# An attention and mixture-of-experts kernel: its opening in another order, the first expert's weights split earlier, list entries of 64 bytes

## The chip, the cores and the metric

One core of a Trainium2 chip runs the whole program. Its engines are TensorE (PE, matmuls), VectorE (DVE), ScalarE (ACT), GpSimd (POOL) and SyncE (SP), which only issues DMAs; ScalarE and GpSimd issue DMAs too. The engines run beside each other and meet at semaphores. The metric is the device time of one launch in microseconds, the median of several runs.

## The reference, cut to what matters

64 images of 224 x 224 x 3 are cut into 196 patches of 768 values and embedded to 192 features; with a class token that is 197 tokens an image, 12608 in all. Then come a causal attention with 12 heads of 16, a residual and a layer norm, and a layer of eight experts with two choices per token and a capacity:

```python
emb = concat([cls, patches(x / 255) @ W + b]) + pos_emb
h = layernorm(emb + attn(emb))                      # 12 heads, causal softmax
scores, idx = top_k(h @ Wg, 2); weights = softmax(scores)
for k in range(2):                                  # capacity = int(1.2 * N / 8)
    pos = cumsum(onehot(idx[:, k])) - 1; keep = pos < capacity
    buf[idx, pos] = token                           # one list of tokens per expert and choice
    xg = h[buf]; a = (xg @ W1)[..., :H] * silu((xg @ W1)[..., H:])
    out[buf] += w_k * (a @ W2)
y = layernorm(h + out)
```

## The kernel before, in words

The program has two blocks, `attention_block` and `expert_block`, with a barrier of all engines between them. Products that need precision split an operand into a rounded part (`_hi`) and the rest (`_lo = value - _hi`): an engine rounds, another subtracts.

**Attention.** Work goes by pairs of images (`NPAIR` = 32), 396 columns each. `run_bodies` calls `body(i, ...)` for i = 0 to 35 on each engine, each body with twelve steps `s`; the middle ones run in a hardware loop. A body works on several pairs at once, by stages: "E" embeds pair i + 1, stage 1 makes q and k of pair i, 2 the scores of i - 1, 3 and on softmax, values and projection, 4 the norm, the choice of experts and the slots of i - 3, 5 the scatter of list entries of i - 4. q and k are stored to DRAM (`store_qk`) and read back in another layout (`spread_q`, `spread_k`) by SP. `embed(p, ft, k0)` on TensorE multiplies six 128-row tiles (`KT`) with three products each, for two halves `ft` of the features, 18 matmuls a half; VectorE's `embedded(p, ft)` turns the sum into `ht`. It needs `x_hi` (ScalarE, `x_round`) and `x_lo` (GpSimd, `x_rest`).

**The opening** (before body 0). SP loads `wtok` (768 KB), `raw` (776 KB), the six tiles of x of pair 0 (198 KB each), `wp` (144 KB) and thirteen constants, in this order. `wtok` and `raw` are loaded into `vp`, the tiles that later hold the values. Everything waits for the last constant (`s_w`): TensorE then does four small products (L574 to L586: the mean of the gate weights, the gate folded into the projection, and bias products), VectorE what hangs on them, ScalarE rounds `wtok`, then `raw`, then x. VectorE subtracts `wtok_lo` and `wa_lo` one after the other (L783, L784), then clears `vp` (L791); TensorE starts to embed when both are ready (`s_wsplit`). ScalarE clears the expert lists in DRAM first of all (L457).

**The lists.** For each token and choice, an entry with the weight and the token's row is written to `d["lists"]` at its slot by an indirect DMA of GpSimd (L443), eight per pair: steps s with s % 3 != 2. There are 30720 slots; an entry has `ROW` = 2 words. GpSimd also raises the variance to -1/2 (`rstd`, L420) at step 4 of each body, and masks the softmax. VectorE's code of step 2 multiplies y by the reciprocals (L840), which come by a DMA from ScalarE.

**Experts.** 80 chunks (`NCH`) of 384 list slots, ten for each expert. For each chunk SP loads the entries (`load_entries`), GpSimd gathers the tokens' rows of 1 KB with three indirect DMAs (L1142), TensorE turns them (`turn_rows`, L1225), ScalarE and VectorE split them, TensorE multiplies (L1242, L1255), and GpSimd scatters the result with an adding DMA (L1162). The weights of an expert (1408 KB) are split in ten pieces (`parts`): GpSimd rounds, VectorE subtracts. For expert 0 all ten stand at the start of the block (L1151, L1331); for the others one piece per chunk. SP loads the raw weights of experts 0 and 1 after the first four loads of entries and `ident`, those of expert x + 2 in chunk 2 of expert x. A last part normalizes all tokens.

## Time and profile before

| what | value |
|---|---|
| runs, median (lowest to highest) | 2357.99 us (2357.78 to 2363.21), 3 runs |
| profiled execution | 2355.76 us |
| its span, first to last instruction | 2354.0 us |
| TensorE busy | 2140.5 us (91%) |
| VectorE, ScalarE, GpSimd busy | 1590.6, 1083.2, 1576.6 us |
| opening, to the first QK product | 36.77 us |
| barrier between the blocks, first load of the experts | 1364.40 us |

A row of the timeline has the start in us, the duration in us, engine, line, operation, output<-input, shape and count, and in brackets the engine's idle time before it and what released it. A row of windows has the stretch, its length, busy time (and count) of the engines, the granted TensorE clock (1.00 is 2.4 GHz, 0.50 is 1.2 GHz), the busy share of the DMA engines and GB/s.

### The profile page before, as it was taken

The numbers are of one execution on the slowest core, as the hardware profiler recorded it, in microseconds if no ns is written. First come the engines' busy times: TensorE is split into PE (matmuls) and PEld (weight loads), VectorE is DVE, ScalarE is ACT, GpSimd is POOL, SyncE is SP. The second block draws the span as 40 slices with busy tenths as digits, with TensorE's granted clock in tenths as the row PEclk, the third lists the DMA queues.
The fourth block names the chain that finished last, engine by engine and source line by source line (L and its number), as shares of the span: only waits on it lengthen the run. The fifth ranks groups of instructions, "written<-read, shape, count | busy, mean of one in ns | idle before, by whom it ended". The sixth has DMA issues, their size and how long they took to land. (4 is left out here: it accounts for less than half of the span.)

```text
span 2354.0 us, 48984 instructions
## 1 busy us (share of the span) xinstructions
PE 2140.5 (91%) x14772; PEld 2070.2 (88%) x14772; DVE 1590.6 (68%) x4287; ACT 1083.2 (46%) x2840; POOL 1576.6 (67%) x2326
## 2 busy tenths in 40 slices
PE   4999999999999999999999559999999999999990
PEld 4899898999989999999988459999999999999980
DVE  4577777877777777777777436666666666666556
ACT  2344444444444444444444225454545454544545
POOL 3356676767666767676765557777777777767666
PEclk9999999999999999999999679999999999999995
DMA  5658888776676565655643133201010101000338
GB/s 155 153 119 123 137 127 142 130 133 137 140 124 139 135 135 136 134 137 133 139 111 84 34 112 62 44 6 26 2 29 3 28 3 26 2 2 15 54 48 332
DMA packets 232530, 219.72 MB, mean 93 GB/s; under 512 B 91027, under 2 KB 212754, under 8 KB 231376
## 3 DMA queue, kind: packets, MB, share of 16 engines
q1 hardware_dynamic: 134800, 146.55, 26.7%
q10 hardware_dynamic: 43328, 56.78, 12.9%
q0 software_dynamic: 54272, 14.76, 5.1%
q8 instruction: 68, 1.11, 0.2%
q14 instruction: 62, 0.51, 0.1%
HBM read 152.91 MB, written 95.25 MB: 105 GB/s over the span
## 5 line engine op out<-in xcount | busy, mean ns | idle before, releaser
L1162 POOL DMA_INDIRECT x_tokens<-yout,e_entry x240 | 382.0, 1592 | 182.1 <-DVE yout L1348 133.5
L651 PE MATMUL Y<-p,vp 128*102 128x198 f32 x1536 | 361.0, 344 | 17.6 <-ACT ysb L482 13.0
L443 POOL DMA_INDIRECT expert_lists<-entry,slot x256 | 288.1, 1126 | 54.1 <-issue 54.1
L1363 DVE TENSOR_TENSOR a<-UP,gate 128x384 f32<-128x384 f32 x320 | 178.6, 558 | 211.7 <-ACT gate L1300 169.8
L487 ACT ACTIVATE p<-ST 128x396 f32<-128x396 f32 x384 | 191.7, 499 | 264.5 <-PE ST L623 247.9
L1255 PE MATMUL Y<-w,a_hi 128*128 128x384 f32 x960 | 304.4, 354 | 2.0 <-DVE a_lo L1353 2.0
L1142 POOL DMA_INDIRECT rows<-x_wide,e_entry x240 | 250.3, 1043 | 77.4 <-issue 72.4
L1300 ACT ACTIVATE gate<-GT 128x384 f32<-128x384 f32 x320 | 157.6, 492 | 290.1 <-PE UP L1242 267.8
L141 POOL TENSOR_TENSOR word_p<-word_p 1x1 f32<-1x1 f32 x416 | 85.8, 206 | 304.6 <-ACT p L489 295.3
L409 POOL TENSOR_TENSOR x_lo<-x,x_hi 128x396 fp32r<-128x396 f32 x192 | 208.2, 1086 | 91.1 <-ACT x_hi L465 89.0
L651 PEld LDWEIGHTS Y<-p,vp 128*102 128x102 f32 x1536 | 221.6, 170 | 32.2 <-issue 11.4
L829 DVE TENSOR_REDUCE rm<-S 128x2 f32<-128x256 f32 x384 | 161.7, 421 | 117.6 <-PE S L642 106.9
L832 DVE TENSOR_REDUCE rm<-S 70x2 f32<-70x396 f32 x384 | 213.9, 557 | 0.0
L629 PE MATMUL S<-k,q 96*128 96x128 f32 x768 | 185.8, 243 | 25.2 <-DVE rm L832 18.6
L1262 PE MATMUL Y<-w,a_lo 128*128 128x192 f32 x960 | 206.8, 256 | 0.0
L655 PE MATMUL Y<-p,vp 70*102 70x70 f32 x1536 | 191.8, 247 | 1.9 <-POOL p L431 1.9
L655 PEld LDWEIGHTS Y<-p,vp 70*102 70x102 f32 x1536 | 185.7, 171 | 3.0 <-POOL p L431 2.6
L629 PEld LDWEIGHTS S<-k,q 96*128 96x128 f32 x768 | 147.4, 192 | 40.4 <-DVE rm L832 28.3
L1255 PEld LDWEIGHTS Y<-w,a_hi 128*128 128x128 f32 x960 | 180.9, 189 | 2.3 <-DVE a_lo L1353 2.2
L849 DVE RECIPROCAL rd<-ysb 6x198 f32<-6x198 f32 x128 | 177.4, 1386 | 4.7 <-ACT ysb L482 0.8
L1348 DVE SCALAR_TENSOR_TENSOR yout<-Y,e_entry,ylo 128x192 f32<-128x192 f32 x240 | 100.3, 418 | 117.0 <-ACT ylo L1289 105.4
L1353 DVE TENSOR_TENSOR a_lo<-a,a_hi 128x384 fp32r<-128x384 f32 x320 | 178.3, 560 | 0.0
(181 smaller groups left out, 6400.1 us busy)
## 6 DMA issues: line engine op xcount, KB each, us to landing
x<-in_xt ACTq DMA_DIRECT2D x180, 198.0 KB
q<-qk_features SPq DMA_DIRECT2D x384, 74.2 KB
k<-qk_features SPq DMA_DIRECT2D x192, 148.5 KB
qk_features<-qk_hi SPq DMA_DIRECT2D x96, 198.0 KB
qk_features<-qk_lo SPq DMA_DIRECT2D x96, 198.0 KB
e_raw<-in_wexp SPq DMA_DIRECT2D x8, 1408.0 KB, 6.7
rb<-rd ACTq DMA_DIRECT2D x128, 74.2 KB
t_x<-x_tokens SPq DMA_DIRECT2D x15, 576.0 KB, 7.5
```

The costliest lines, as they stand in the source:

```text
L409: pool.tensor_tensor(x_lo[:, t], x[:, t], x_hi[:, t].bitcast(F32), ALU.subtract)\
L443: pool.indirect_dma_start(d["lists"][:, :], bass.IndirectOffsetOnAxis(ap=slot[o][0:REAL[t], t, c:c + 1], axis=0), entry[o][0:REAL[t], t, c ...
L487: act.activation(p32[b][:, :, 0:TI], ST[0][:, 0:TP].rearrange("p (h c) -> p h c", h=2), ACT.Exp, scale=SCALE)
L629: pe.matmul(S[0][:, b * P:(b + 1) * P], qt[rows, im, b, j, 0:P], kt[rows, im, j, 0:P], start=(b == 0), stop=False)
L651: return pe.matmul(Y[0:VW1, 0:TI], v0, p32[b][:, hh, 0:TI], start=start, stop=stop)
L655: pe.matmul(Y[0:VW1, P:TI], v1, p32[b][0:T1, hh, TI:TI + T1], start=False, stop=False)
L832: dve.tensor_reduce(rm[im][0:T1, 1, j:j + 7:6], S[1][0:T1, 0:TP].rearrange("p (h c) -> p h c", h=2), AX.X, ALU.max, negate=True).then_inc( ...
L1142: pool.indirect_dma_start(rows[cc % 2][:, t, :], None, d["xin"][:, :], row_of(cc, t), bounds_check=N - 1, oob_is_err=False).then_inc(s_row ...
L1162: pool.indirect_dma_start(d["x1"][:, :], row_of(cc, t), yout[q][:], None, bounds_check=N - 1, oob_is_err=False, compute_op=ALU.add)\
L1255: return pe.matmul(y[:, 0:2 * C], a_hi[q][:, m, c], w2[e][:, m].rearrange("p a b -> p (a b)"), start=(m == 0), stop=(m == HM - 1))
L1262: pe.matmul(y[:, 0:C], a_lo[q][:, m, c], w2[e][:, m, 0], start=False, stop=False)
L1363: dve.tensor_tensor(a32[m % 2][:], UP[m % 2][:, 0:TILE3], gate[m % 2][:], ALU.mult)\
```

## The change

Three edits are made together.

- **The opening.** SP loads wtok, the x of pair 0, raw, and seven constants that are needed later; `wp` and the other seven constants go by ScalarE's queue. wtok has its own semaphore. ScalarE rounds wtok and x before `raw`, and clears the lists last. VectorE subtracts `wtok_lo` first, and `wa_lo` only after the first half of the embedding. TensorE embeds the first half before the small products, which then stand between the parts of the second half. One of the two clearings of q goes to GpSimd, and the clearing of `vp` into body 0 at step 6.
- **The first expert's weights.** Tiles that attention no longer needs (x, x_hi, x_lo, ht, wtok_lo) become the first of the two sets of expert weights. SP loads the first expert's weights at the end of body 32; ScalarE rounds and VectorE subtracts them in body 34 at step 0. In that body GpSimd's `rstd` moves from step 4 to step 11. At the start of the expert block SP loads one expert's weights instead of two, and no second `ident`.
- **The entries** have 16 words (64 bytes) instead of 2; the lists grow from 240 KB to 1920 KB, and are cleared from a tile that is written ten times.

```diff
+ROW, BLANK = 16, 24
 XW = C + C - P
...
-        x = sb("x", [P, KT, TP], F32)
-        x_hi, x_lo = (sb(n, [P, KT, TP], F32R) for n in ("x_hi", "x_lo"))
...
-        loads = [(wpt, "wpt"), (wg, "wg"), (bpc, "bpc"), (bqk, "bqk"), (bv, "bv"), (bp, "bp"), (postab, "pos"),
-                 (biastab, "bias"), (ident, "ident"), (masks, "masks"), (iota8, "iota8"),
-                 (kbase, "kbase"), (valid, "valid"), (tid, "tid")]
+        loads = [(wpt, "wpt"), (wg, "wg"), (bpc, "bpc"), (bv, "bv"), (bp, "bp"), (postab, "pos"), (biastab, "bias")]
+        late_loads = [(bqk, "bqk"), (ident, "ident"), (masks, "masks"), (iota8, "iota8"), (kbase, "kbase"),
+                      (valid, "valid"), (tid, "tid")]
...
-            sp.dma_start(wtok, d["wtok"]).then_inc(s_w, 16)
-            sp.dma_start(raw, d["raw"]).then_inc(s_w, 16)
+            sp.dma_start(wtok, d["wtok"]).then_inc(s_tok, 16)
             for t in range(KT):
                 sp.dma_start(x[:, t], d["xt"][0][:, t]).then_inc(s_x, 16)
-            sp.dma_start(wp[0:CH, :, E:], d["wp"]).then_inc(s_w, 16)
-            for dst, name in loads:
+            sp.dma_start(raw, d["raw"]).then_inc(s_w, 16)
+            for dst, name in late_loads:
                 sp.dma_start(dst[:], d[name]).then_inc(s_w, 16)
...
+                if isinstance(i, int) and i == NPAIR:
+                    sp.wait_ge(s_ef, 2 * NPAIR)
+                    sp.wait_ge(s_xlo, KT * NPAIR)
+                    sp.wait_ge(s_hlo, 2 * NPAIR)
+                    shared.load_weights(sp, d, 0, 0)
...
+            pool.memset(q[1][:].bitcast(F32), 0.0).then_inc(s_qset, 1)
...
-                    if s == 4 and 4 in stages:
+                    if s == (11 if isinstance(i, int) and i == NPAIR + 2 else 4) and 4 in stages:
...
-            act.wait_ge(s_blank, 1)
-            act.dma_start(d["lists"].rearrange("(p a) c -> p (a c)", p=P),
-                          blank[:].rearrange("p a c -> p (a c)")).then_inc(s_clear, 16)
-            act.wait_ge(s_w, 16 * (len(loads) + 3))
+            act.dma_start(wp[0:CH, :, E:], d["wp"]).then_inc(s_w, 16)
+            for dst, name in loads:
+                act.dma_start(dst[:], d[name]).then_inc(s_w, 16)
+            act.wait_ge(s_tok, 16)
             act.activation(wtok_hi[:], wtok, ACT.Copy).then_inc(s_whi, 1)
-            act.wait_ge(s_wg, 2)
-            act.activation(wa_hi[:].rearrange("p a b -> p (a b)"), raw, ACT.Copy).then_inc(s_whi, 1)
...
+            act.wait_ge(s_w, LOADS)
+            act.wait_ge(s_wg, 2)
+            act.activation(wa_hi[:].rearrange("p a b -> p (a b)"), raw, ACT.Copy).then_inc(s_whi, 1)
+            act.wait_ge(s_blank, 1)
+            act.dma_start(d["lists"].rearrange("(p n a) c -> p n (a c)", p=P, a=BLANK),
+                          blank[:].rearrange("p a c -> p (a c)").unsqueeze(1)
+                          .broadcast_to([P, NSLOT // P // BLANK, BLANK * ROW])).then_inc(s_clear, 16)
...
+                            if isinstance(i, int) and i == 1:
+                                act.wait_ge(s_vset, 4)
...
+                    if isinstance(i, int) and i == NPAIR + 2 and s == 0:
+                        act.wait_ge(shared.s_raw[0], 48)
+                        for j in range(10):
+                            src, hi, _ = shared.parts(j, 0)
+                            act.activation(hi, src, ACT.Copy).then_inc(shared.s_whi, 1)
...
-            pe.wait_ge(s_w, 16 * (len(loads) + 3))
-            pe.wait_ge(s_set, SETS)
...
-            pe.wait_ge(s_wsplit, 1)
...
-            for ft in range(2):
-                for k0 in range(0, KT, 2):
-                    embed(0, ft, k0)
+            pe.wait_ge(s_toksplit, 1)
+            for k0 in range(0, KT, 2):
+                embed(0, 0, k0)
+            pe.wait_ge(s_w, LOADS)
+            pe.wait_ge(s_set, SETS)
+            for f in range(2):
+                mm = pe.matmul(G[0][:, 0:E], share[:], wg[:, f, :], start=(f == 0), stop=(f == 1))
+            mm.then_inc(s_avg, 1)
+            embed(0, 1, 0)
...
+            embed(0, 1, 2)
...
+            embed(0, 1, 4)
+            pe.wait_ge(s_wsplit, 1)
...
+            dve.memset(q[0][:].bitcast(F32), 0.0).then_inc(s_qset, 1)
             for n in range(2):
-                dve.memset(q[n][:].bitcast(F32), 0.0).then_inc(s_qset, 1)
+                dve.memset(y[n][CH:CH + 1, 0, :], 1.0).then_inc(s_qset, 1)
+            dve.wait_ge(s_whi, 1)
+            dve.tensor_tensor(wtok_lo[:], wtok, wtok_hi[:].bitcast(F32), ALU.subtract).then_inc(s_toksplit, 1)
             for n in range(2):
                 ins = dve.memset(k[n][ROWS_QK:ROWS_QK + 1].bitcast(F32), 1.0)
             ins.then_inc(s_qset, 1)
-            for n in range(2):
-                dve.memset(y[n][CH:CH + 1, 0, :], 1.0).then_inc(s_qset, 1)
-            dve.wait_ge(s_w, 16 * (len(loads) + 3))
+            dve.wait_ge(s_w, LOADS)
             dve.tensor_tensor(addend[:], postab[:], biastab[:], ALU.add).then_inc(s_const, 1)
             dve.tensor_copy(bvs[:], bv[:].unsqueeze(2).broadcast_to([CH, 2, P])).then_inc(s_const, 1)
             dve.tensor_copy(bps[:], bpc[:].unsqueeze(2).broadcast_to([CH, 2, P])).then_inc(s_const, 1)
+            dve.wait_ge(s_const, 1)
+            embedded(0, 0)
             dve.wait_ge(s_avg, 1)
             gates = raw.rearrange("p (a b) -> p a b", a=2)[:, :, 3 * C:3 * C + E]
             dve.tensor_tensor(gates, gates, repeat(G[0][:, 0:E], 2), ALU.subtract).then_inc(s_wg, 1)
...
-            dve.tensor_tensor(wtok_lo[:], wtok, wtok_hi[:].bitcast(F32), ALU.subtract)
...
-            dve.wait_ge(s_wsplit, 1)
-            for n in range(2):
-                dve.memset(vp[n][:], 0.0).then_inc(s_vset, 1)
-            dve.wait_ge(s_vset, 2)
-            for n in range(2):
-                dve.memset(bass.AP(vp[n], CH, [[KV, P], [6 * VW1, 4], [VW1 + 1, 6]]), 1.0).then_inc(s_vset, 1)
...
-            embedded(0, 0)
...
+                    if isinstance(i, int) and i == 0 and s == 6:
+                        dve.wait_ge(s_wsplit, 1)
+                        dve.wait_ge(s_toksplit, 1)
+                        for n in range(2):
+                            dve.memset(vp[n][:], 0.0).then_inc(s_vset, 1)
+                        dve.wait_ge(s_vset, 2)
+                        for n in range(2):
+                            dve.memset(bass.AP(vp[n], CH, [[KV, P], [6 * VW1, 4], [VW1 + 1, 6]]), 1.0)\
+                                .then_inc(s_vset, 1)
...
+                    if isinstance(i, int) and i == NPAIR + 2 and s == 0:
+                        for j in range(10):
+                            dve.wait_ge(shared.s_whi, j + 1)
+                            src, hi, lo = shared.parts(j, 0)
+                            dve.tensor_tensor(lo, src, hi.bitcast(F32), ALU.subtract).then_inc(shared.s_wlo, 1)
...
-            sp.dma_start(ident[:], d["ident"]).then_inc(s_id, 16)
-            for e in range(2):
-                sp.dma_start(raw[e][:], d["wexp"][e]).then_inc(s_raw[e], 16)
+            load_weights(sp, d, 1, 1)
...
-                    sp.dma_start(raw[x % 2][:], d["wexp"][x + 2]).then_inc(s_raw[x % 2], 16)
+                    load_weights(sp, d, x + 2, x % 2)
...
-            pool.wait_ge(s_raw[0], 16)
-            for j in range(10):
-                src, hi, _ = parts(j, 0)
-                pool.tensor_copy(hi, src).then_inc(s_whi, 1)
...
-            for j in range(10):
-                split_piece(j + 1, j, 0)
...
+        raw1 = [flat(x, n1), None]
+        raw2 = [[t[:, 0:n2 // 2] for t in ht], None]
+        self.w1_hi = [flat(x_hi, n1).rearrange("p (a b) -> p a b", a=2)]
+        self.w1_lo = [flat(x_lo, n1).rearrange("p (a b) -> p a b", a=2)]
+        self.w2 = [flat(wtok_lo, 2 * n2).rearrange("p (m a c) -> p m a c", m=HM, a=2)]
...
+    def load_weights(self, sp, d, expert, e):
+        n1, n2 = 2 * 2 * HID, HM * C // 2
+        sp.dma_start(self.raw1[e], d["wexp"][expert][:, 0:n1]).then_inc(self.s_raw[e], 16)
+        for n in range(2):
+            cols = slice(n1 + n * n2, n1 + (n + 1) * n2)
+            sp.dma_start(self.raw2[e][n], d["wexp"][expert][:, cols]).then_inc(self.s_raw[e], 16)
```

On VectorE, the opening before, from the weight subtractions to the first bodies:

```order
L783 TENSOR_TENSOR wtok_lo<-vp,wtok_hi 128x1536
L784 TENSOR_TENSOR wa_lo<-vp,wa_hi 128x1552
L788 TENSOR_TENSOR wp<-G,bp 1x200
L791 MEMSET vp 128x2448 x2
L794 MEMSET vp 128x4x6 x2
L804 SCALAR_TENSOR_TENSOR ht<-EB,addend 128x396 x2
L854 TENSOR_TENSOR h_lo<-ht,h_hi 128x396
```

And on VectorE after, from the first subtraction on:

```order
L795 TENSOR_TENSOR wtok_lo<-vp,wtok_hi 128x1536
L797 MEMSET k 1x2376 x2
L800 TENSOR_TENSOR addend<-postab,biastab 128x396
L801 COPY bv_columns<-bv 96x256
L802 COPY bp_wide<-bp_columns 96x256
L785 SCALAR_TENSOR_TENSOR ht<-EB,addend 128x396
L807 TENSOR_TENSOR vp<-vp,G 128x2x8
L808 TENSOR_TENSOR wg_centred<-wg,G 96x16
L810 COPY wp<-G 96x2x8
L813 TENSOR_TENSOR wa_lo<-vp,wa_hi 128x1552
```

The first ht now stands ahead of the centred gates and of wa_lo, and the memsets of vp have left the opening.

On ScalarE, the opening before (the first row clears the lists):

```order
L457 DMA expert_lists<-blank 128x480
L460 ACT_TABLE_LOAD
L460 ACTIVATE wtok_hi<-vp 128x1536
L462 ACTIVATE wa_hi<-vp 128x1552
L465 ACTIVATE x_hi<-x 128x396 x6
```

And after:

```order
L461 DMA postab<-in_pos 128x396
L461 DMA biastab<-in_bias 128x396
L463 ACT_TABLE_LOAD
L463 ACTIVATE wtok_hi<-vp 128x1536
L466 ACTIVATE x_hi<-x 128x396 x6
L473 ACTIVATE wa_hi<-vp 128x1552
L475 DMA expert_lists<-blank 1280x1x384
```

x is rounded before raw (wa_hi), and the clearing of the lists, larger, has gone behind both.

On GpSimd, from the last scatters of list entries over the barrier (L202) to the first expert chunks, before:

```order
L443 DMA expert_lists<-entry,slot 30720x2 x3
L420 TENSOR_TENSOR rstd<-rstd,half 128x4
L423 TENSOR_TENSOR shift<-mv,rstd 128x4
L443 DMA expert_lists<-entry,slot 30720x2 x5
L141 TENSOR_TENSOR word_p<-word_p 1x1
L443 DMA expert_lists<-entry,slot 30720x2 x8
L202 UNCONDITIONAL_BRANCH
L1131 UNCONDITIONAL_BRANCH
L1134 MEMSET rows 128x768 x2
L1135 MEMSET t_half 128x6
L1142 DMA rows<-x_wide,e_entry 128x256 x3
L1151 CAST w_hi<-e_raw 128x256 x8
```

And after:

```order
L446 DMA expert_lists<-entry,slot 30720x16 x8
L423 TENSOR_TENSOR rstd<-rstd,half 128x4
L426 TENSOR_TENSOR shift<-mv,rstd 128x4
L141 TENSOR_TENSOR word_p<-word_p 1x1
L446 DMA expert_lists<-entry,slot 30720x16 x8
L202 UNCONDITIONAL_BRANCH
L1133 UNCONDITIONAL_BRANCH
L1136 MEMSET rows 128x768 x2
L1137 MEMSET t_half 128x6
L1144 DMA rows<-x_wide,e_entry 128x256 x9
```

Five scatters have moved ahead of rstd, and the casts of the first expert's weights no longer stand between the gathers of the first chunks.

## Rows read from the trace of the kernel before

**Rows 1.** Windows of the trace, one stretch in the middle of the attention loop:
```profile
1200.00:1240.00 40.00, 38.87 (x299) 37.28 (x298) 30.18 (x92) 18.41 (x54) 25.83 (x55) 1.00 0.45 105
```

**Rows 2.** Windows of the opening, TensorE alone: small products, then the first embedding:
```profile
15.00:22.00 7.00, 4.83 (x20) 1.00 0.00 0
24.00:31.00 7.00, 6.07 (x18) 1.00 0.65 174
```

**Rows 3.** Timeline of the opening, TensorE:
```profile
31.43 0.45 PE L605 MATMUL EB<-x_hi,wtok_hi 128*128 128x396 f32 x1 [0.78 <-DVE ht L804]
...
36.77 0.45 PE L593 MATMUL G<-h_hi,wa_hi 128*128 128x396 f32 x1 [1.83 <-DVE h L857]
```

**Rows 4.** Timeline of the opening, ScalarE, VectorE and GpSimd:
```profile
18.95 2.21 ACT L465 ACTIVATE x_hi<-x 128x396 fp32r<-128x396 f32 x5
19.15 1.75 DVE L783 TENSOR_TENSOR wtok_lo<-vp,wtok_hi 128x1536 fp32r<-128x1536 f32 x1
19.54 3.92 POOL L409 TENSOR_TENSOR x_lo<-x,x_hi 128x396 fp32r<-128x396 f32 x1 [15.76 <-ACT x_hi L465]
23.42 3.00 POOL L409 TENSOR_TENSOR x_lo<-x,x_hi 128x396 fp32r<-128x396 f32 x3
```

**Rows 5.** Windows of the opening, all engines, while the inputs are loaded:
```profile
2.00:10.00 8.00, 0.00 (x0) 0.00 (x0) 7.06 (x2) 1.28 (x1) 1.73 (x8) 1.00 0.96 352
```

**Rows 6.** Timeline of VectorE, a memset of vp and pair 1's ht:
```profile
23.55 2.10 DVE L791 MEMSET vp<- 128x2448 f32 x1 [0.57 <-issue]
...
47.56 0.57 DVE L804 SCALAR_TENSOR_TENSOR ht<-EB,addend 128x396 f32<-128x396 f32 x1 [3.29 <-PE EB L605]
```

**Rows 7.** Waits of TensorE from 40 to 80 us: total, times, longest:
```profile
PE S L629 <- DMA k<-qk_features: 6.0, 1, 6.0
```

**Rows 8.** Timeline of the end of attention, GpSimd and VectorE:
```profile
1328.29 1.00 POOL L443 DMA_INDIRECT expert_lists<-entry,slot  x1 [0.54 <-issue]
...
1333.31 0.36 DVE L840 TENSOR_TENSOR y<-ysb,rb 96x198 f32<-96x198 f32 x1 [4.21 <-DMA rb<-rd]
...
1339.61 1.05 POOL L420 TENSOR_TENSOR rstd<-rstd,half 128x4 f32<-128x4 f32 x1 [7.54 <-DVE rstd L894]
...
1344.98 0.16 DVE L964 TENSOR_TENSOR entry<-ex,entry 128x4 f32<-128x4 f32 x1
...
1348.73 1.01 POOL L443 DMA_INDIRECT expert_lists<-entry,slot  x1 [0.15 <-issue]
...
1358.37 1.17 POOL L443 DMA_INDIRECT expert_lists<-entry,slot  x1 [0.30 <-issue]
```

**Rows 9.** Source line of the barrier, GpSimd's branch behind its last wait (start last):
```profile
L202 POOLq COMPARE_BRANCH  x1: 53/53/53, 1360.9 to 1360.9; - x1
```

**Rows 10.** Timeline of VectorE's weight subtractions, beside GpSimd's copies and alone:
```profile
1373.73 4.44 DVE L1331 TENSOR_TENSOR w_lo<-e_raw,w_hi 128x256 fp32r<-128x256 f32 x8 [28.59 <-POOL w_hi L1151]
1378.09 1.32 DVE L1331 TENSOR_TENSOR w<-e_raw,w 128x384 fp32r<-128x384 f32 x2
...
1395.07 0.41 DVE L1331 TENSOR_TENSOR w_lo<-e_raw,w_hi 128x256 fp32r<-128x256 f32 x1
```

**Rows 11.** Timeline of the start of the experts, GpSimd and TensorE:
```profile
1369.75 1.00 POOL L1142 DMA_INDIRECT rows<-x_wide,e_entry  x1 [0.30 <-issue]
...
1377.63 1.51 PE L1225 MATMUL XT<-e_ident,rows 128*128 128x128 f32 x6 [34.70 <-DMA rows<-x_wide,e_entry]
1381.28 0.69 PE L1242 MATMUL GT<-ex_hi,w_hi 128*128 128x384 f32 x1 [2.13 <-DVE ex L1340]
...
1388.94 0.88 PE L1225 MATMUL XT<-e_ident,rows 128*128 128x128 f32 x6 [2.06 <-DMA rows<-x_wide,e_entry]
```

**Rows 12.** Windows of the start of the experts, all engines:
```profile
1370.00:1376.00 6.00, 0.00 (x0) 0.00 (x0) 2.27 (x5) 0.00 (x0) 3.46 (x7) 0.50 1.01 415
```

**Rows 13.** The page's costliest groups, two of GpSimd's: busy, mean ns | idle before:
```profile
L1162 POOL DMA_INDIRECT x_tokens<-yout,e_entry x240 | 382.0, 1592 | 182.1 <-DVE yout L1348 133.5
...
L443 POOL DMA_INDIRECT expert_lists<-entry,slot x256 | 288.1, 1126 | 54.1 <-issue 54.1
```

More of the change, by code:

```diff
@@ L55 @@
 NSLOT = E * K2 * SEG
-ROW = 2
+ROW, BLANK = 16, 24
 XW = C + C - P
@@ L207, in sem @@
             return ctx.enter_context(nc.semaphore(name))
-        wtok_hi, wtok_lo = (sb(n, [P, KT, 2 * P], F32R) for n in ("wtok_hi", "wtok_lo"))
+        wtok_hi, wtok_lo, x, x_hi, x_lo, ht, ident = shared.tiles
         wa_hi, wa_lo = sb("wa_hi", [P, 2, WA], F32R), sb("wa_lo", [P, 2, WA], F32R)
@@ L971, in _, with expert_block @@
             run_bodies(dve, body)
-def expert_block(nc, d, out):
+def expert_block(nc, d, out, shared):
     CPE = K2 * SEG // TILE3
@@ L1400, in build @@
     d["lists"] = nc.dram_tensor("expert_lists", [NSLOT, ROW], F32).ap()
-    attention_block(nc, d)
-    expert_block(nc, d, out)
+    with ExitStack() as ctx:
+        shared = Shared(nc, ctx)
+        attention_block(nc, d, shared)
+        shared.second_set(nc, ctx)
+        expert_block(nc, d, out, shared)
 def kernel(x, L0_tok_W, L0_tok_b, L0_tok_class_token, L0_tok_pos_emb, L0_attn_w_attn,
```

118 lines of the change are left out of this document (66 added, 52 removed).

## The prediction, written before the changed kernel was timed

> **What bounds the kernel now.** I read the busy times by stage first. In the middle of the attention loop TensorE works 38.87 of 40 us [rows 1]: the loop is bound by TensorE, and an edit there has to disturb TensorE to matter. What can be won lies where TensorE stands still: before the first QK product, and between the last attention product and the first expert. There one reads single rows in order of time.
>
> In the opening TensorE first does the small products on gate and projection, 4.83 us of work, then waits, then embeds pair 0. The first half (18 matmuls) takes 6.07 us, 0.337 each [rows 2], and ends at 30.65 (31.43 less 0.78 of idle); the second half runs from 31.43 to 34.94 (36.77 less 1.83 of idle), 0.195 each; QK starts at 36.77 [rows 3]. The column of the granted clock reads 1.00 throughout, but 0.337 for 396 columns is the pitch of 1.2 GHz, and 0.195 is near that of 2.4; I go by the pitch. The first half waits for x_lo, which GpSimd computes: its first piece takes 3.92 us, the later ones 1.00 (three in 3.00). The long one lies under VectorE's subtractions of the weights, the first of two being wtok_lo, 1.75 us from 19.15 [rows 4].
>
> At the end of attention y is ready at 1333.67, rstd comes at 1339.61 and the entries of the last pair are ready at 1345.14 (1344.98 + 0.16). Yet their first scatter starts at 1348.73, because five scatters of the pair before stand behind rstd and ahead of it. The last starts at 1358.37 [rows 8] and has landed by 1360.9 [rows 9]. The expert stage then gathers the first chunk's rows, the third gather at 1369.75, while the raw weights of two experts (2 x 1.44 MB) fill the DMA engines [rows 12]. TensorE turns the rows at 1377.63, multiplies from 1381.28, and waits again, 2.06 us, for the second chunk's rows at 1388.94 [rows 11].
>
> **The opening.** wtok and x now head SP's queue, and half of the constants go by ScalarE's. From 2 to 10 us the DMA engines moved 352 GB/s, 2.8 MB [rows 5]. wtok (0.79), x (1.22) and all that ScalarE's queue carries (0.81) are 2.8 MB, so x is there by about 10.0 even if the queues share evenly, and wtok by 6.6. Its rounding is four times a piece of x (2.21 for five, rows 4), 1.7, and wtok_lo 1.75: ready by 10.1. x_lo starts 0.59 after x_hi does (18.95 to 19.54), at 10.6; nothing with two inputs runs on VectorE then, since wa_lo now comes after the first half. Six pieces at 1.00 end at 16.6; before, 19.54 + 3.92 + 4.9 = 28.4.
>
> The first half ended 2.25 us after the last x_lo (30.65 - 28.4): now 18.9. The raw weights and late constants are the same bytes as before, which were there when the small products began, by 15.3 at the latest [rows 2], so they hold nothing up. Then the small products, hidden until now, lie on the path: 4.83. The second half adds 3.5 at the fast pitch, 6.1 at the slow. From 12.6 TensorE has no gap (six matmuls, 2.02 us, match two x_lo), and before, the fast pitch came after some 6 us of such work; so I take it. 18.9 + 4.83 + 3.5 = 27.2, and QK follows 1.83 later at 29.0: **7.7 us earlier**. With the slow pitch it is 5.2; with the small products at half their time too, 10.1.
>
> New waits there: VectorE waits for the first half before it centres the gates, and ScalarE waits for the gates before wa_hi, with the clearing of the lists and h_hi behind. They are over by about 21, so wa_lo ends by 26, ahead of the 27.2 that TensorE needs. GpSimd's memset of q[1] is over before x is there: 2448 elements of vp took VectorE 2.10 [rows 6], so 4752 are about 4.1.
>
> Moved behind: the memsets of vp (2 x 2.10, with gaps 4.9) now stand on VectorE between qk_lo and the ht of pair 1. In the old order's times that is from 44.3 (47.56 less 3.29 of idle), so ht is late by 1.6 [rows 6]. TensorE waits 6.0 us in that stretch for k to be spread by DMA [rows 7]; that hides it, and without the cover it would cost 1.6. The clearing, now 1.97 MB for 0.25, is issued at about 22, takes 5.6 us at 352 GB/s, and is over before QK's results are stored. If it met them it would cost up to 5.6.
>
> **The end of attention.** The first expert's weights are loaded after pair 29's stores, some 35 us before use; only stores stand behind that load. ScalarE rounds ten pieces, and VectorE subtracts them in the 4.21 us in which it waits for the reciprocals ahead of y [rows 8]. A 256-wide subtraction takes 0.41 alone and 0.555 beside GpSimd's copies [rows 10]. Eight such and two of 384 are 3.8 us pipelined, 5.8 at the worst (4.44 + 1.32); they begin about 1 us into the gap, so y is late by 0.6 to 2.6. I take 1.2, nearer to the lone row, for the scatters beside it are no copies. On GpSimd the five scatters move ahead of rstd: from 1332.1 (1339.61 less 7.54 idle), at 1.3 to 1.4 each, they end at 1339.1, before the variance is there. The last pair's scatters then start 0.9 after their entries (0.54 of idle behind the word of 0.18, as at 1328.29) instead of 3.6: 2.7 less 1.2, **1.5 us**; ends -0.5 and 2.1.
>
> The 64-byte entries: the landing after the last scatter is at most 1.4 us (1360.9 - 1359.5) [rows 8, 9], which bounds a gain. A gather of rows of 1 KB takes GpSimd 1.00, a scatter of 8 bytes 1.126 [rows 11, 13], so bytes hardly set it: zero, between -1 and +1.
>
> **The start of the experts.** 1.44 MB no longer stand before the first gathers. At 415 GB/s [rows 12] that is 3.5 us, so the rows are turned 3.5 us sooner after the stage begins. It can't be over 5, as the third gather ends at 1370.75 and must land. GpSimd's ten casts are gone, so the second chunk's gathers go out before the next weights are loaded, and the 2.06 us go too. **5.5 us**; ends 4.5 and 7. Next late is the chain of turning, rounding and subtracting, 3.65 us (1377.63 to 1381.28), which stays.
>
> The sum is 7.7 + 1.5 + 5.5 = 14.7. The profiled execution took 2355.76 (span 2354.0), which becomes 2341.1. It lies 2.2 below the median of the runs, 2357.99, so the forecast for the median is **2343.3**.
>
> **A rule against it.** GpSimd's first x_lo shows VectorE costing it 2.9 us in 3.5 us of subtractions with two inputs in SBUF [rows 4]. The Trainium skill (GPSIMD Engine Reference, 1. Specifications) makes that general: GpSimd shares its SBUF interfaces with VectorE and contends with instructions that have two SBUF inputs. The split now stands beside the scatters; by the rule they would be up to 2.9 us late and the sum 12.8, by my reading of the scatters 14.7. It is part of rival 2.
>
> **Rivals.** (1) The DMAs of the first bodies give the start back: the clearing, or pair 1's x, pushes the QK stores and the spreading. For it: TensorE's start there hangs on a DMA [rows 7]. Against: the clearing should be over. It takes back 5.6 to 7.7: 2348.9 to 2351. (2) The second half stays at the slow pitch, and the starved scatters make rstd late: 14.7 - 2.5 - 1.9 = 10.3, 2347.7. (3) Slower: a scatter of 64 bytes takes GpSimd longer in the loop. The dearest indirect DMA is the adding one, 1.592, 0.466 more [rows 13]; eight a pair, 3.7 us, are 119 over 32 pairs: 2462. If all is exposed, it decides from 0.057 us a scatter (14.7 over 256). Against it stand the 1 KB gathers at 1.00. (4) The change doesn't do what it says at the experts: the first gathers land as late as before, and the second wait stays. 7.7 + 1.5 = 9.2, 2348.8.
>
> **How the numbers follow.** Forecast, 2339 to 2346.5: 0.58. Rival 2 and its like, to 2349: 0.17. Rivals 1 and 4, 2348.5 to 2353: 0.14. Rival 3 or another loss in the loop, above 2365: 0.05. All terms at their upper ends, below 2339: 0.06. A measurement can tell about 0.3%, 7.1 us: faster is below 2350.9. A half of rivals 1 and 4 and a little of a raised median lie above it: faster 0.83, same 0.12, slower 0.05. The range of 2336.5 to 2351 leaves out the far ends.
>
> **What would show it.** Right: a first x_lo of 1.0 us, embedding from about 12.6 and QK from about 29; the last pair's first scatter within 1 us of its entries; rows turned about 14.6 instead of 18.1 us after the last scatter's end, with no wait at the second turning; TensorE as busy in the loop. Wrong: an embedding that waits for wtok or x, a second half at 0.337, QK stores behind the clearing, a rstd that waits for scatters, scatters above 1.2 us in the loop.

## The result: twice the forecast gain, 11 to 15 us of it from the step put at zero

| what | before | after |
|---|---|---|
| median of the runs | 2360.6 us (2357.78 to 2365.08, 4 runs) | 2327.41 us (2324.15 to 2330.54, 4 runs) |
| ratio, 95% interval | | 0.9859 (0.9839 to 0.9878) |
| span of the profiled execution | 2354.0 | 2322.4 |
| TensorE busy | 2140.5 | 2134.6 |

The forecast was 2343.3, a gain of 14.7 us. The medians above differ by 33.2 us, the profiled executions by 31.6, and in a second set of runs (e5 below) the medians by 29.3.

**Opening.** The timeline of the changed kernel (columns as in the prediction's rows: start, duration, engine, line, operation):

```profile
10.73 2.65 ACT L466 ACTIVATE x_hi<-x 128x396 fp32r<-128x396 f32 x6 [2.61 <-DMA x<-in_xt]
11.35 6.34 POOL L412 TENSOR_TENSOR x_lo<-x,x_hi 128x396 fp32r<-128x396 f32 x6 [3.73 <-ACT x_hi L466]
13.50 0.67 PE L601 MATMUL EB<-x_hi,wtok_hi 128*128 128x396 f32 x1 [13.50 <-POOL x_lo L412]
19.09 0.51 PE L612 MATMUL G<-wg,share 96*128 96x8 f32 x4
19.99 0.45 PE L601 MATMUL EB<-x_hi,wtok_hi 128*128 128x396 f32 x1 [0.39 <-DVE ht L785]
21.18 0.77 PE L618 MATMUL G<-wg_centred,wp_turned 96*96 96x8 f32 x8
22.96 0.84 PE L624 MATMUL G<-wp,bv_columns 96*128 96x200 f32 x4
27.35 0.42 PE L589 MATMUL G<-h_hi,wa_hi 128*128 128x396 f32 x1 [2.02 <-DVE h L869]
```

QK starts at 27.35 instead of 36.77 [rows 3], 9.4 us earlier. x_lo takes 1.06 a piece and no longer a first 3.92 [rows 4]; the small products stand between the parts of the second half and take 2.63 us of work, with four more of 0.51 at L626, instead of 4.83 [rows 2].

**End of attention, start of the experts.** The timeline of the changed kernel, GpSimd, VectorE and TensorE:

```profile
1307.01 2.92 POOL L446 DMA_INDIRECT expert_lists<-entry,slot  x1 [0.30 <-issue]
1308.52 0.36 DVE L852 TENSOR_TENSOR y<-ysb,rb 96x198 f32<-96x198 f32 x1
1315.49 1.06 POOL L423 TENSOR_TENSOR rstd<-rstd,half 128x4 f32<-128x4 f32 x1
1321.22 1.05 POOL L446 DMA_INDIRECT expert_lists<-entry,slot  x1 [0.55 <-issue]
1330.89 1.17 POOL L446 DMA_INDIRECT expert_lists<-entry,slot  x1 [0.30 <-issue]
1346.22 1.54 PE L1220 MATMUL XT<-ident,rows 128*128 128x128 f32 x6 [28.08 <-DMA rows<-x_wide,e_entry]
1354.82 0.82 PE L1220 MATMUL XT<-ident,rows 128*128 128x128 f32 x6
```

From y to the last pair's first scatter there are 12.70 us instead of 15.42 [rows 8], from the end of the last scatter (1332.06) to the first turning 14.2 instead of 18.1, and to the second, which waits for nothing now, 22.8 instead of 29.4 [rows 8, 11].

**The loop.** It was not to change, and it gave the most. rstd of pair 0 comes at 136.95 before and 127.03 after, rstd of pair 26 at 1164.52 and 1138.21: the lead grows from 9.9 to 26.3 us. (It is 24.8 at the last y, 34.1 at the second turning of rows and 31.6 at the end.) The page shows where it grows. Its line of the DMA engines' busy share in 40 slices of the span, in tenths, of before:

```profile
DMA  5658888776676565655643133201010101000338
```

And of after:

```profile
DMA  7656565656565656565644143201010101001338
```

Before, the engines are at 8 tenths from slice 4 to 7 and calm down later, with the same work in every body. Windows from one rstd to the next (pairs 3 to 6), columns as in rows 2, TensorE alone, of before:

```profile
215.12:256.11 40.99, 38.86 (x288) 1.00 0.90 135
256.11:298.11 42.00, 39.99 (x288) 0.96 0.76 132
298.11:337.12 39.01, 38.07 (x288) 1.00 0.85 136
337.12:378.72 41.60, 38.18 (x287) 1.00 0.89 129
```

And of after:

```profile
204.35:243.00 38.65, 37.97 (x287) 1.00 0.63 139
243.00:282.44 39.44, 38.12 (x288) 1.00 0.59 137
282.44:321.35 38.91, 38.02 (x288) 1.00 0.60 137
321.35:360.25 38.90, 38.03 (x287) 1.00 0.61 136
```

The bytes per second are nearly the same (last column: 129 to 136 against 136 to 139); the engines were busy 0.3 to 0.5 longer in moving them (0.76 to 0.90 against 0.59 to 0.63), and some bodies took 41 to 43 us instead of 38.9. Four such bodies, the three here and one of 42.69 at 692, hold 11.4 us of the 16.4; of the others most are 0.1 to 0.3 longer than after.

### The profile page after: what moved, and what is told of

Same layout as the page of the kernel before. It is cut to its first block and busy times, and to the rows that moved or that the text cites. A ratio compares the mean times of both kernels' runs of the same rounds, so it can differ in the third digit from the quotient of the medians.

```text
span 2322.4 us, 49007 instructions
## 1 busy us (share of the span) xinstructions
PE 2134.6 (92%) x14772; PEld 2068.0 (89%) x14772; DVE 1578.2 (68%) x4286; ACT 1084.3 (47%) x2850; POOL 1577.8 (68%) x2317
## 5 line engine op out<-in xcount | busy, mean ns | idle before, releaser
L668 PE MATMUL Y<-p,vp 128*102 128x198 f32 x1536 | 360.9, 344 | 14.8 <-ACT ysb L490 8.8
L1284 ACT ACTIVATE ylo<-Y,e_entry 128x192 f32<-128x192 f32 x240 | 101.2, 422 | 159.7 <-PE Y L1250 159.7
L430 POOL TENSOR_SCALAR_AFFINE_SELECT p<-p 128x256 f32<-128x256 f32 x384 | 170.5, 444 | 0.0
L652 PE MATMUL S<-k,q 96*70 96x198 f32 x768 | 166.5, 259 | 0.0
```

The source lines that it names most:

```text
L668: return pe.matmul(Y[0:VW1, 0:TI], v0, p32[b][:, hh, 0:TI], start=start, stop=stop)
```

## Experiments 1: which part made the loop quicker

Theories: **A**, 8-byte entries in DRAM slow the other DMAs; **B**, the new opening's timing; **C**, the size of the lists' tensor moves others in DRAM. Four kernels, timed together with the kernel before (27 runs, median 2352.01).

**e1**, the kernel before with the entries alone:

```diff
-ROW = 2
+ROW, BLANK = 16, 24
```

> The kernel before with entries of 16 words instead of 2, and with the clearing of the lists issued by ScalarE behind the rounding of x; opening and experts as before. Theory A (the 8-byte entries slowed the other DMAs of the attention loop, and with them TensorE): in the two traces the distance between the rstd of the same pair grew from 9.9 to 25.5 us over the loop, so this kernel alone gains about 16 us over the kernel before, and the DMA engines' busy share between 215 and 418 us falls from 0.8 to about 0.6. Theory B (the loop's gain comes from the opening's other timing against the DMAs): no difference, at most 2 us. The prediction's own term: between -1 and +1 us.

Measured: 2341.85, ratio 0.9951 (0.9935 to 0.9968). Of 16 us 10 (by the medians) to 11.5 (by the ratio) came. The DMA engines' share from 215 to 418 us is 0.60, against 0.84 in the kernel before. In its trace the lead over the kernel before is 15.3 us at pair 26, as A says, and 10.9 at the end; the last bodies gave some back (below).

**e2**, the changed kernel with 8-byte entries again:

```diff
-ROW, BLANK = 16, 24
+ROW, BLANK = 2, 240
```

> The changed kernel with entries of 2 words again (the clearing, 240 KB, from a tile written once): opening and weight split stay. Theory A: it loses the 16 us of the loop and keeps the opening's 9.4 and the 5.9 of the end of attention and the experts' start: about 2343.5. Theory B: within 2 us of the changed kernel, 2327.

Measured: 2341.61, ratio 0.9949 (0.9930 to 0.9968). The slow bodies are back: 43.01, 42.90 and 44.65 us, those that end at rstd of pairs 3, 4 and 6. B falls. TensorE's timeline in the last of them, and its windows around it:

```profile
366.14 0.34 PE L589 MATMUL G<-h,wa_lo 128*128 128x396 f32 x1
369.97 0.49 PE L634 MATMUL ST<-q,k 97*128 97x396 f32 x1 [3.48 <-DMA q<-nm]
```

```profile
357.00:363.00 6.00, 5.92 (x46) 1.00 0.83 140
363.00:369.00 6.00, 3.18 (x21) 1.00 0.97 127
369.00:375.00 6.00, 5.03 (x25) 0.72 0.89 157
375.00:381.00 6.00, 6.00 (x47) 1.00 0.49 96
```

This slow body has two parts. TensorE waits 3.5 us for a small DMA (`nm` into q, 9 KB) behind DMA engines that are busy all the time (0.97); right after the wait the granted clock falls to the lower level (0.72 as a mean): 25 matmuls in 5.03 us of busy time, 46 in 5.92 before. The whole body is 5.7 us late: 3.5 by the wait, and most of the rest by the clock, which is low for the 3.4 us from 370.23 on. Not every slow body has both: in the kernel before, that of 41.60 us has a wait of 2.4 us for the same DMA at a clock of 1.00, and that of 42.69 one of 2.9 us for VectorE's `rm`.

**e3**, the changed kernel, entries 64 bytes apart but only 8 bytes of each written:

```diff
+        lists8 = d["lists"].rearrange("n (a c) -> (n a) c", c=2)
...
-                            d["lists"][:, :],
+                            lists8,
...
-                            entry[o][0:REAL[t], t, c, :], None,
-                            bounds_check=NSLOT - 1
+                            entry[o][0:REAL[t], t, c, 0:2], None,
+                            bounds_check=8 * NSLOT - 1
...
-                        ch.mark(dve.tensor_tensor(slot[o][:], sl[:], over[:], ALU.add))
+                        ch.mark(dve.scalar_tensor_tensor(out=slot[o][:], in0=sl[:], scalar=8.0, in1=over[:],
+                                                         op0=ALU.mult, op1=ALU.add))
```

> The changed kernel with the entries still 64 bytes apart in DRAM, but with only their first 8 bytes written (slots times 8, rows of 2 words). If it is the neighbourhood of 8-byte entries within one line of memory that costs (theory A1): as the changed kernel, 2327. If it is the width of the write, the part of a line that has to be merged (theory A2): as with 8-byte entries, about 2343.5.

Measured: 2326.84, ratio 0.9884 (0.9860 to 0.9908), no slow body. The width of the write is not it (A2 falls). The Trainium skill (DMA: Bandwidth & Descriptors, Specifications) says that below 512 bytes a DMA does read-modify-write and loses line rate; by that rule on size, 8 and 64 bytes would be alike, packed or apart. What separates the kernels here is the distance of the entries, which the rule does not speak of: 8 bytes packed bring the slow bodies (e2), 8 bytes 64 apart do not.

**e4**, 8-byte entries packed, in a tensor eight times as large:

```diff
-    d["lists"] = nc.dram_tensor("expert_lists", [NSLOT, ROW], F32).ap()
+    d["lists"] = nc.dram_tensor("expert_lists", [8 * NSLOT, ROW], F32).ap()[0:NSLOT]
```

> The changed kernel with entries of 2 words packed as before, but in a tensor of 1920 KB of which the first eighth is used. If the size of the tensor, and where that puts the others in DRAM, made the gain (theory C): 2327. If the entries did (theory A): as the changed kernel with 8-byte entries, about 2343.5.

Measured: 2338.94, ratio 0.9944 (0.9924 to 0.9964), bodies of 43.63 and 43.94 us. C falls.

## Experiments 2: what each of the three parts is worth

Timed together (before: 11 runs, 2353.06). **e5** is the changed kernel itself.

> The changed kernel itself, beside the next three. If the three parts add, it gains over the kernel before what the entries alone gained in the first set of runs (a ratio of 0.9951, 11.5 us) and what opening and weights together gained there (0.9949, 12.0 us): 23.5 us, a ratio of 0.9900. If the entries are worth more once the opening is new (the larger gain of the first comparison, 0.9859), 0.986.

Measured: 2323.74, ratio 0.9880 (0.9863 to 0.9897): 29.3 us, between the two that were expected.

**e6**, the opening as before, the rest changed (the diff is the opening's part, taken back).

> The changed kernel with the opening of the kernel before; entries of 64 bytes and the earlier weight split stay. The first QK product comes at 36.3 instead of 27.4 us. If that lead is kept to the end: 9.4 us slower than the changed kernel. If something in the loop takes it back (rival 1 of the prediction): less than 4 us slower.

Measured: 2333.79, 10.1 us slower than e5. QK starts at 36.55 (27.52 in e5), 9.0 us later; at rstd of pair 0 e5 leads by 8.2 us and at pair 26 by 8.4. About 1 us is thus lost before pair 0's rstd and nothing in the loop: rival 1, which takes 5.6 to 7.7 back, falls.

**e7**, the weight split taken back:

```diff
-            load_weights(sp, d, 1, 1)
+            for e in range(2):
+                load_weights(sp, d, e, e)
...
+            for j in range(10):
+                src, hi, _ = parts(j, 0)
+                pool.tensor_copy(hi, src).then_inc(s_whi, 1)
```

> The changed kernel without the earlier split: both experts' weights are loaded after the barrier, GpSimd rounds and VectorE subtracts the first expert's there, rstd of body 34 is back at step 4. By the two traces the split was worth 2.0 us at the end of attention and 3.9 at the first turning of rows, 6.6 by the second: 6 to 8 us slower than the changed kernel. The last pair's first scatter starts 3.6 us after its entries, the block's start to the first turning takes 13.2 us instead of 9.4. By the prediction's terms (1.5 and 5.5): 7.0.

Measured: 2331.9, 8.2 us slower than e5. Its first turning of rows comes 16.6 us after the last scatter's end, the second 27.3 (13.97 and 23.9 in e5). Taking the split back costs 2.6 us at the first turning and 3.4 at the second, less than the 3.9 and 6.6 between the kernel before and the changed one. e7 keeps the weights' load in three parts and still leaves out the second `ident`; whether these make the rest was not run.

So opening 10.1, split 8.2, and what is left of 29.3 for the entries is 11.0. In the first set it was 14.8 (e2 against e3). The runs of one kernel have a standard deviation of mostly 2 to 5 us, which leaves a difference of two medians of six runs unsure by 4 to 5 us (resampling the runs, at 95%).

## Experiments 3: distance of the entries, or place of the tiles

**e8**, entries of 32 bytes (timed with e5 to e7):

```diff
-ROW, BLANK = 16, 24
+ROW, BLANK = 8, 60
```

> The changed kernel with entries of 8 words, 32 bytes apart, so that two share 64 bytes. If the packets are held up by neighbours inside 64 bytes: packets over 1 us between 300 and 600 us return (11 with 64 bytes, 627 with 8), and the time rises by some 4 to 15 us. If 32 bytes are far enough: as the changed kernel.

Measured: 2330.28, 6.5 us slower than e5, and yet only 9 long packets (10 in e5): the time came by another way. Every pair took 39.07 instead of 38.90 (234.44 and 233.40 us for six). With 16 words the tile `blank` had shrunk from 480 words to 384, so all tiles of SBUF behind it had moved. That made theory **D**, that the tiles' place sets the pace of the pairs, against **E**, that the entries in DRAM do. Four kernels (before: 11 runs, 2347.02):

**e9**, the changed kernel with the tiles pushed back:

```diff
         blank = sb("blank", [P, BLANK, ROW], F32)
+        sb("room", [P, 96], F32)
```

> The changed kernel with 96 unused words of SBUF behind the tile that clears the lists. With entries of 64 bytes that tile has 384 words, in the kernel before and with 32 bytes it has 480, so all tiles behind it moved by 384 bytes. In the traces ScalarE's instructions of the loop are 1 to 3 ns shorter with 384 words (p 497 against 499, vp 329 against 331), TensorE waits less for ysb (1.2 against 2.3 us in six pairs), and a pair takes 38.90 instead of 39.05 us. Theory D (the place of the tiles makes this): pairs of 39.05 again, about 3.5 to 4 us slower than the changed kernel, and no long packets. Theory E (the entries in DRAM make it): 38.90, no difference.

Measured: 2330.54, ratio 0.9919 (0.9897 to 0.9941), 7.6 us slower than e10 below, where 3.5 to 4 were expected (resampling: 1.0 to 10.3). Six pairs in the middle of the loop, windows of TensorE, of e5 and of e9:

```profile
827.68:1061.08 233.40, 228.09 (x1718) 1.00 0.60 136
```

```profile
829.11:1063.26 234.15, 228.18 (x1717) 1.00 0.60 136
```

The same matmuls take the same time; 0.12 us a pair is idle time between them. Waits of TensorE over six pairs (total, times, longest), of e5 and of e8, which has the slow pace too:

```profile
PE Y L668 <- ACT ysb L490: 1.2, 7, 0.2
```

```profile
PE Y L668 <- ACT ysb L490: 2.3, 8, 0.4
```

**e10, e11, e12**: entries of 32, 16 and 8 bytes, with unused words behind `blank` and `entry` so that every tile stays where the changed kernel has it. e12:

```diff
-ROW, BLANK = 16, 24
+ROW, BLANK = 2, 120
...
+        sb("room", [P, 144], F32)
...
+        sb("room_entry", [P, 224], F32)
```

> Entries of 8 words (32 bytes), with every tile where the changed kernel has it. Theory D: pairs of 38.90, as the changed kernel (2323.7), 6.5 us faster than the kernel with 32 bytes measured before. Theory E: pairs of 39.05, 4 to 6 us slower than the changed kernel. Few packets over 1 us by both.

> Entries of 4 words (16 bytes), tiles as in the changed kernel. Packets over 1 us between 300 and 600 us: 627 with 8 bytes, 9 with 32. If neighbours within 32 bytes hold the DMAs up, there are some hundreds here, and the time lies between the changed kernel and 8-byte entries, 3 to 8 us slower. If only 8 bytes do it: as the changed kernel.

> Entries of 8 bytes, tiles as in the changed kernel: the long packets alone, without the other place of the tiles. Theory D: with them the loss is what is left of the 14.8 us between 8 and 64 bytes once 3.5 to 4 us for the tiles are taken off: about 11 us slower than the changed kernel; pairs after 800 us at 38.90. Theory E: 14.8 us slower, pairs after 800 us at 39.05.

Measured: e10 2322.98, e11 2324.12, e12 2327.24; all three at 38.90 a pair after 800 us. D holds and E falls: 32 bytes, 6.5 us slower than e5 with the tiles moved, is no slower with the tiles in place. e11 has 224 long packets and still is only 1.1 us slower than e10, below the 3 to 8 expected and inside the noise. Theory D had 11 us for the neighbours in e12, and 4.3 came (against e10; resampling: 0.2 to 9.5), in part because the place had been put at 3.5 to 4 and measured 7.6. With this opening the two, 4.3 and 7.6, make 11.9, about the whole of the entries' 11.0 to 14.8.

The distance of the entries shows in the DMA queues' lines (packets, MB, share of 16 engines' time) for 300 to 600 us, of the kernel before, e12 (8 bytes), e11 (16) and e5 (64); q1 is SP's queue, q10 is ScalarE's:

```profile
q1 hardware_dynamic: 27611, 28.90, 48.9%
q10 hardware_dynamic: 10044, 11.75, 28.3%
```

```profile
q1 hardware_dynamic: 28061, 29.08, 44.7%
q10 hardware_dynamic: 9933, 11.53, 26.7%
```

```profile
q1 hardware_dynamic: 27671, 28.59, 38.9%
q10 hardware_dynamic: 10045, 11.76, 21.5%
```

```profile
q1 hardware_dynamic: 27830, 28.71, 39.1%
q10 hardware_dynamic: 10105, 11.80, 19.0%
```

And in the number of packets of the trace that took over 1 us (the expectations count the same from a clock that starts some 10 us earlier, hence 627):

```
entries                          300 to 600 us    800 to 1200 us
before, 8 bytes                       622               31
e12, 8 bytes                          476               17
e11, 16 bytes                         224               18
e10, 32 bytes                           4               18
e5, 64 bytes                           10               16
e3, 8 bytes, 64 apart                  17               19
```

Entries less than 32 bytes from each other hold up other DMAs. Of the 622 packets of the kernel before, 273 are of 1584 bytes on ScalarE's queue, which brings x, and 310 of 4752 bytes on SP's, which stores and spreads q and k; neither queue touches the lists there. In that kernel, where scatters go out at 300.40, 305.65 and 308.57 us, packets of 1584 bytes, 0.07 us at the median, took up to 3.92 us (one that starts at 307.71). How a scatter holds them up, in the DMA engines or in DRAM, no run shows. After about 730 us the long packets stop, although the scatters go on: in the six traces with 8 or 16 bytes the last burst lies at 694 to 731 us, 4 us ahead of rstd of pair 15 in five of them and 15 us in e11. So it hangs on how far the work has come; no run told why.

Nor does a long packet always cost TensorE time. Bodies of 41 us or more ahead of the loop's end: 4 in the kernel before (with that of 40.99), 3 in e2 and 2 in e4 (8 bytes, the old place of the tiles), 1 in e12, none in e13 below (8 bytes, tiles moved) and none in e11; none in any trace with entries 32 bytes or more apart.

## Experiments 4: the old opening, and which tiles

**e13**, the kernel before, 8-byte entries, the tiles moved and, as in e1 and e17, the clearing of the lists issued behind the rounding of x (before: 17 runs, 2345.99; the diff without the clearing and the words behind `entry`).

```diff
-        blank = sb("blank", [P, NSLOT // P, ROW], F32)
+        blank = sb("blank", [P, BLANK, ROW], F32)
+        sb("room", [P, 144], F32)
```

> The kernel before with its 8-byte entries, but with the tiles of SBUF where entries of 64 bytes put them (the tile that clears the lists 384 words instead of 480, unused words behind the entries), and the clearing issued behind the rounding of x. Theory D: the place of the tiles is worth in the kernel before what it is in the changed one (2330.5 against 2323.0): pairs of 38.90 instead of 39.05, about 6 to 8 us faster than the kernel before; the long packets (627 over 1 us between 300 and 600 us) stay, and with them a few bodies of 41 to 43 us. Entries of 64 bytes alone gained 11.5, so that 4 are left for the neighbours in DRAM. If the gain of the 64-byte entries in the kernel before was the neighbours' alone: no difference here.

Measured: 2345.47, ratio 0.9993 (0.9979 to 1.0007). A miss: 6 to 8 were expected, none came. The pairs did take 38.92 and the long packets stayed (513), but no body of 41 to 43 us did. The body at the loop's end takes 45.71 at a clock of 0.89; in the one trace of the kernel before it takes 42.07 at 1.00. Windows of that body, of e13 and of the kernel before:

```profile
1148.85:1194.56 45.71, 42.81 (x291) 0.89 0.49 112
```

```profile
1164.52:1206.59 42.07, 38.89 (x290) 1.00 0.51 119
```

These 3.6 us are about what the quicker pairs had brought (0.12 us each). That this is why nothing came is not shown: the profiled execution of e13 is one of its fastest (2340.02), its span is 15.7 us shorter than that of the kernel before, while the medians are level, and the kernel before has one trace. With the old opening and 64 bytes the body is long too (46.13 in e1, 4.1 of what e1 gave back; 44.93 in e17, 43.44 in e6); with the new opening it is not in any trace (41.5 to 42.4).

**e17**, the kernel before with 64-byte entries and the tiles left in place (before: 17 runs, 2352.85).

```diff
-ROW = 2
+ROW, BLANK = 16, 30
```

> The kernel before with entries of 64 bytes, and the clearing tile of 480 words, so that the tiles up to the entries stay where the kernel before has them. It closes the square on the old opening: 8-byte entries with the tiles moved gave 0.9993 of the kernel before, 64-byte entries with the tiles moved 0.9951. If neighbours in DRAM are the whole of the gain on the old opening: pairs of 39.05 us, hardly any packet over 1 us, 0.995 again. If both changes are needed there: 0.998 to 1.000.

Measured: 2343.59, ratio 0.9960 (0.9943 to 0.9977), 9.3 us; 39.02 a pair, 13 long packets, 44.93 at the loop's end. On the old opening, then, the distance of the entries is worth 9 to 10 us (e17 against the kernel before, e1 against e13) and the place of the tiles nothing that can be measured. What each of the two is worth thus depends on the opening; their sum is 11 to 12 on both. Where e13 loses its 10 us against e1 its one trace doesn't show: from 215 to 418 us TensorE works 198.61 us in both, at a DMA share of 0.77 in e13 and 0.60 in e1.

**e14, e15, e18**: the changed kernel with 96 unused words behind `p32`, and with 128 and 64 behind `blank`, one run each.

```diff
         p32 = [sb(f"p32_{n}", [P, 2, TI + T1], F32) for n in range(3)]
+        sb("room", [P, 96], F32)
```

> The changed kernel with the 96 unused words behind p32 instead of behind the clearing tile: q, k, vp, hres, rm, nm and p32 stay, and ysb, rd, rb, y, r and all behind move by 384 bytes. If the pace hangs on a tile up to p32 (most of ScalarE's longer instructions write p, vp or hres): pairs of 38.90. If it hangs on one behind: 39.05, as with all moved.

> The changed kernel with 128 unused words (512 bytes) behind the clearing tile, where 96 gave pairs of 39.05. If tiles want a place on a multiple of 128, 256 or 512 bytes of what they have now: 38.90. If any shift does it: 39.05.

> The changed kernel with 64 unused words (256 bytes) behind the clearing tile. 384 bytes gave pairs of 39.05 us, 512 bytes 38.90. If the place counts modulo 256 bytes: 38.90. If modulo 512: 39.05 or a third value.

Measured, six pairs in the middle: e14 234.04 (slow pace), e15 233.41, e18 233.35 (quick). So moving q, k, vp, hres and p32 as well adds nothing (234.15 in e9), a tile from `ysb` on matters, and in these moves its place counts modulo 256 bytes: moves by 256 and 512 bytes leave the pace, a move by 384 costs it. The times of these single runs, 2324.35, 2326.24 and 2324.5, don't tell the two paces apart. Which tile it is stays open.

## Experiment 5: rstd at step 4 again

**e16**, one run:

```diff
-                    if s == (11 if isinstance(i, int) and i == NPAIR + 2 else 4) and 4 in stages:
+                    if s == 4 and 4 in stages:
```

> The changed kernel with rstd of body 34 back at step 4, ahead of five scatters, while the weights are still split in that body. The prediction put 2.7 us on moving it and took 1.2 back for the split beside it. Here rstd comes without waiting for scatters (in the changed kernel 0.8 us late), but the last pair's first scatter is again behind five: it starts 2 to 3.5 us after its entries instead of 0.9, and the block of the experts starts 1 to 2 us later, counted from y.

Its timeline, VectorE and GpSimd:

```profile
1310.60 0.35 DVE L852 TENSOR_TENSOR y<-ysb,rb 96x198 f32<-96x198 f32 x1
1316.89 1.04 POOL L423 TENSOR_TENSOR rstd<-rstd,half 128x4 f32<-128x4 f32 x1 [8.11 <-DVE rstd L906]
1326.01 1.01 POOL L446 DMA_INDIRECT expert_lists<-entry,slot  x1 [0.16 <-issue]
```

From y to the first scatter: 15.41 us, against 12.70 with rstd moved. The move is worth 2.7, as the prediction had it, and more than the 1 to 2 expected of this run: the scatter starts 3.6 us after its entries. The single time, 2325.16, doesn't resolve that.

## Why the prediction was wrong, by its own steps

**The 64-byte entries** are the step that failed: "bytes hardly set it: zero, between -1 and +1". It was bounded by what the scatter costs GpSimd, which was right (a mean of 1.134 us after, 1.126 before, so rival 3 had nothing to stand on), and by the landing at the very end. That a scatter could hold up the DMAs of other queues had no term, nor had the move of the tiles. Measured: 11 to 15 us, of two causes. Neighbours in DRAM cost 4.3 us with the new opening (unsure: 0.2 to 9.5) and 9 to 10 with the old opening. The tiles' place, which no line of the diff names, is 7.6 by the medians of e9 and e10 and 6.5 by their spans, of which the slower pace explains the 3.0 that lie in the loop up to pair 26; on the old opening it is nothing. All terms at their upper ends make 20.2 us, so that no mix of them reaches the measured 29 to 33. The two reasons given for looking no further were weak. [rows 1] is one window at 1200 us, where the DMA share is 0.45, and stood for a loop whose share was 0.90 at 215 us. And "TensorE as busy in the loop" was a sign to look for, but the only rivals in the loop were losses; a gain there had no price.

**The opening**, 7.7 forecast, 10.1 timed and 9.4 in the trace. The first half ended at 19.1, as forecast (18.9), though by two errors that cancel: x was there at 10.7 and not 10.0, and its last five matmuls ran at the quick pitch already. The term mis-sized is the small products, "now they lie on the path: 4.83". From 19.09 to the end of the second half (27.35 less 2.02) are 6.2 us, of which the second half alone is 3.5, as before, so the small ones and their one wait took 2.7. They ran at the higher clock here, at the lower one in the kernel before. The text had this as its upper end, 10.1. That the first half's end came out right is luck.

**The end of attention and the experts' start**, 7.0 forecast, 8.2 timed. The move of rstd gave its 2.7 (e16). The split made y late by 0.7 (from GpSimd's word behind the entries of the pair before to y 6.43 us, before 5.74), where 1.2 was taken: 2.0 net instead of 1.5. (The lower end given for it, -0.5, does not follow: 2.7 less 2.6 is 0.1.) The rows are turned 3.9 us sooner, not 3.5, and at the second turning the lead is 6.6 instead of 5.5; against e7 it is 2.6 and 3.4, so that by e7's trace the split and the move make 5.4 us and not 8.2. The timed 8.2 is unsure by 4 to 5 and does not decide. At the end of the program 2.5 us less are left of the lead than at the second turning: from the last chunk's output products to the end it takes 68.7 us after and 66.5 before, and anything from 66.0 to 68.9 over all twenty traces, whatever the kernel.

**The rule on GpSimd and VectorE.** Beside the split one scatter took 2.92 us instead of 1.17 to 1.31, so by that rule of the Trainium skill (GPSIMD Engine Reference, 1. Specifications) the trace agrees. In seven of the fourteen traces with the split and the later rstd that scatter takes 2.91 to 2.92, in the other seven 1.36 to 1.37; what decides it is open. It cost nothing: where it is long rstd comes 7.0 us after the last y instead of 6.3, but the last entries are ready 11.7 us and the first scatter starts 12.7 us after y in all fourteen.

**Rivals.** 1 fell with e6. Of 2 the slow pitch did not come, and the starved scatter made rstd 0.8 late instead of 1.9 and cost nothing. 3 and 4 did not come. Opening and split alone, as forecast, would have given 14.7; with 8-byte entries in the old place they timed at 10.4 (e2), with 64-byte entries at 18.3, so that the slow bodies may also have taken a part of what these two parts bring; 10.4 and 18.3 come from two sets of runs, and this is not shown.

## What to carry to other kernels

Small scattered writes are to be priced by what they do to other queues, not by their issue: compare the DMA engines' busy share at equal bytes per second over the whole span, and if it is higher where scatters run, set the entries 32 bytes or more apart. What that is worth is to be timed: 224 long packets cost 1.1 us (e11), some 500 cost 4 to 10. When a tile changes its size, all tiles behind it move; keep the old addresses with unused words when an edit is to be judged, and try a move by itself (here 384 bytes cost the pace, 256 and 512 did not; 128 was not run). A wait of TensorE in a tight loop can cost more than itself (3.5 us cost 5.7 in e2), when the clock falls behind it.

## What the runs showed of the hardware

- 8-byte entries next to each other, scattered by GpSimd, made packets of other DMAs take over 1 us 476 to 622 times in 300 us; 16 bytes apart 224 times; from 32 bytes on 4 to 17 times. It depends on the distance, not on the width of the write (e3).
- The effect stopped by itself at 694 to 731 us, just ahead of rstd of pair 15, in all six kernels with 8 and 16 bytes.
- Moving small tiles of SBUF by 384 bytes costs 0.11 to 0.17 us of a pair's 38.9 (e14, e9, e8), by 256 or 512 bytes nothing (e18, e15); single instructions of ScalarE differ by 1 to 3 ns (p 497 against 499 in the pages of after and before).
- The granted clock also fell in two bodies in which TensorE stands still for some 3 us anyway, the one at the loop's end (45.7 us at 0.89 in e13, otherwise 42.1 at 1.00) and that of pair 30 (35.8 at 0.86 in e3, otherwise 31.5), in some traces and not in others.
- The median of the kernel before lay between 2346 and 2361 us in six sets of runs. Such clock falls and the number of slow bodies are the likely reason; with one trace of that kernel it is not shown.
